# A recommendation tower on one core: one first load, a transposed batch in another PSUM bank, filler matmuls, layer 3 ahead of the dots, and gathers held behind lookups, dots and layer 1

## The reference, cut to what matters

```python
e = stack([tbl_0[ids[:, 0]], ..., tbl_25[ids[:, 25]]], axis=1)      # 512 x 26 x 128
sd = einsum('bfd,bd->bf', e, dense)
ss = einsum('bfd,bgd->bfg', e, e)
z = concatenate([dense, sd, ss[:, iu, ju]], axis=1)                 # pairs with f < g
h = concatenate([z, dense], axis=1)                                 # 512 x 607
h = maximum(h @ W_top1 + b_top1, 0.0)                               # 512 hidden
h = maximum(h @ W_top2 + b_top2, 0.0)                               # 256 hidden
y = h @ W_top3
```

## Time and profile before

| | us |
|---|---|
| median of 3 runs (lowest, highest) | 152.84 (150.93, 153.49) |
| time of the profiled execution | 151.2 |
| its span | 149.4 |
| mean granted TensorE clock | 0.886 |
| busy: PE, PE weight loads | 108.6, 95.6 |
| busy: DVE, ACT, POOL | 79.9, 66.7, 66.0 |
| DMA, mean over the span | 83 GB/s, 12.35 MB |

### The profile page before, as it was taken

The page is one execution under the profiler, slowest core; times in us unless marked ns, Lnnn a source line. Parts: engine busy times, 40 slices in busy tenths (PEclk is TensorE's granted clock), DMA queues, the critical chain, the costliest instruction groups (busy, mean ns, idle before and its releaser), DMA issues.

```text
span 149.4 us, 2760 instructions
## 1 busy us (share of the span) xinstructions
PE 108.6 (73%) x1074; PEld 95.6 (64%) x1074; DVE 79.9 (53%) x217; ACT 66.7 (45%) x151; POOL 66.0 (44%) x66
## 2 busy tenths in 40 slices
PE   7799961999999925500001957958997999799794
PEld 7588831888888805400001947948986998699782
DVE  5699919979999274000750020680386189248401
ACT  4463309737786053000502041693398288145620
POOL 7787747768787778777783752000000000000000
PEclk9999996599999996855555699996999999999999
DMA  4877961576999422111120211000000000000000
GB/s 116 257 193 188 247 191 36 175 183 199 305 287 249 153 53 53 53 53 53 35 52 19 57 35 42 2 0 4 4 0 0 4 0 0 4 4 0 0 0 1
DMA packets 5030, 12.35 MB, mean 83 GB/s; under 512 B 1725, under 2 KB 1853, under 8 KB 5018
## 3 DMA queue, kind: packets, MB, share of 16 engines
q1 hardware_dynamic: 3002, 8.09, 18.8%
q0 software_dynamic: 1920, 3.94, 10.3%
q10 hardware_dynamic: 96, 0.15, 0.4%
HBM read 12.18 MB, written 0.00 MB: 82 GB/s over the span
## 4 chain that ended last, share of the span: by engine, by line
PE 47%; issue 16%; DVE 14%; another core or an unknown queue 13%; ACT 9%; ACTq 0%
PE dots L443 19%; DVE pairs L347 12%; PE dots L487 12%; PE hidden L512 4%; PE hidden L542 3%; PE turned L467 3%; ACT embT L310 2%; ACT high L299 2%; PE dots L421 2%; ACT embT L285 2%; ACT pairs L285 2%; PE turned L512 1%; DVE embT L347 1%; PE last_layers L535 1%
## 5 line engine op out<-in xcount | busy, mean ns | idle before, releaser
L249 POOL DMA_INDIRECT rows<-tbl,gather_idx x60 | 63.3, 1055 | 24.2 <-issue 16.5
L354 DVE TENSOR_SCALAR onehot<-ids_h 125x512 fp32r<-125x512 f16 x88 | 33.4, 435 | 22.5 <-issue 13.9
L443 PE MATMUL dots<-onehot,high 125*128 125x512 f32 (+1 forms) x88 | 36.0, 426 | 0.0
L347 DVE COPY pairs<-dots 27x128 f32<-27x128 f32 (+8 forms) x88 | 23.7, 270 | 21.7 <-PE dots L487 19.1
L467 PE MATMUL turned<-ident,rows 128*128 128x128 f32 x60 | 10.8, 305 | 31.7 <-ACT embT L285 21.5
L443 PE MATMUL dots<-onehot,low 125*128 125x512 f32 (+1 forms) x88 | 32.9, 389 | 0.3 <-issue 0.3
L467 PEld LDWEIGHTS turned<-ident,rows 128*128 128x128 f32 x60 | 7.6, 154 | 34.8 <-issue 34.1
L285 ACT COPY pairs<-dots 27x128 f32<-27x128 f32 (+8 forms) x88 | 20.9, 237 | 18.6 <-PE dots L487 16.6
L299 ACT CAST high<-table 125x1024 fp32r<-125x1024 f32 (+1 forms) x12 | 11.6, 979 | 34.8 <-issue 14.3
L443 PEld LDWEIGHTS dots<-onehot,high 125*128 125x128 f32 x88 | 19.0, 216 | 3.1
L487 PE MATMUL dots<-embT 128*64 128x54 f32 x512 | 17.6, 234 | 3.7 <-DVE pairs L347 2.0
(11 more groups left out here) (43 smaller groups left out, 74.2 us busy)
## 6 DMA issues: line engine op xcount, KB each, us to landing
table<-tbl SPq DMA_DIRECT2D x10, 448.0 KB
wp<-w_pairs SPq DMA_DIRECT2D x2, 512.0 KB
rows<-tbl,gather_idx POOLq DMA_INDIRECT x60
table<-tbl SPq DMA_DIRECT2D x10, 52.0 KB
wd<-w_dense SPq DMA_DIRECT2D x1, 512.0 KB
w2s<-w SPq DMA_DIRECT2D x1, 512.0 KB
table<-tbl SPq DMA_DIRECT2D x2, 224.0 KB
denseT<-dense_t SPq DMA_DIRECT2D x1, 256.0 KB
```

Of the source, the lines that this page charges most:

```text
L249: pool.indirect_dma_start(out=rows[:, t % 2, n, :], out_offset=None, in_=tables[GATHERED_TABLES[n]][:, :], in_offset=bass.IndirectOffsetOn ...
L347: return nc.vector.tensor_copy(dst, src)
L354: nc.vector.tensor_scalar(onehot[:, i % 2, c, :], ids_h[:, i, :], float(c), None, ALU.is_equal).then_inc(onehot_ready, 1)
L443: last = nc.tensor.matmul(selected[t % 2][:, samples], part[:, t % 2, c, :], onehot[:, t % 2, c, samples], start=(part is high and c == 0) ...
```

## The change

- `spread` and the ids of the one-hots lie in one array, `first_needed`, and come with one DMA of 32 rows into one tile `first`; before there were two DMAs.
- Gathers: k = 9 to 41 wait for `table_selected` >= (k-6)//3. k = 42 and 46 also wait for the dots of tile 0, 51 and 54 for those of tile 1, 57 for layer 1 of tile 0. The waits on `transposed` in tiles 2 and 3 stay.
- Batch B2.2 (`APART`) is transposed into `last_layers` instead of `turned`, as soon as table 9's second half has been placed, and goes ahead of D1, as does a step W14 of 14 dummy matmuls. B2.3 and B3.0 move up one place too. `PLACERS` gives batches B2.0, B2.2, B3.0, B3.2, B3.3 to DVE (before: B2.0, B2.3, B3.2, B3.3).
- Y0 goes from behind D2 to ahead of it, Y1 from behind D3 to ahead of it.
- DVE fills `pairs` with ones after the sum of the dense weights in step T10, before at the start.
- The dummy matmuls write `last_layers` instead of `hidden[0]`.

```diff
+SPREAD_WORDS = len(ONEHOT_TABLES) * ROW_PARTS // 2 + 1
...
-    GATHERS_AHEAD, GATHERS_PER_TABLE = 7, 3
+    GATHERS_AHEAD, GATHERS_PER_TABLE = 6, 3
+
+    LATER_GATHERS = GATHERS_AHEAD + GATHERS_PER_TABLE * (N_ONEHOT + 1)
+    HELD_BY_DOTS, HELD_BY_LAYER1 = {42: 1, 46: 1, 51: 2, 54: 2}, {57: 2}
...
-        ids_i = sb("ids_i", [ID_ROWS, BATCH], I32)
+        first = sb("first", [128, BATCH + SPREAD_WORDS], I32)
+        ids_i = first[0:ID_ROWS, 0:BATCH]
...
-        spread_f = sb("spread_f", [128, N_ONEHOT, ROW_PARTS], F16)
+        spread_f = first[:, BATCH:BATCH + SPREAD_WORDS].bitcast(F16)
...
-            T10.0 B2.0 T9.3 T9.4 D0 C0.0 T10.1 T10.2 T10.3 T10.4 C0.1 P0 B2.1 P1
-            D1 C1.0 B2.2 L0.0 L0.1 R0 C1.1 B2.3 M0
-            B3.0 D2 C2.0 Y0 B3.1 L1.0 L1.1 R1 C2.1 P2 B3.2 M1
-            B3.3 D3 C3.0 Y1 L2.0 L2.1 R2 C3.1 P3 M2
+            T10.0 B2.0 T9.3 T9.4 D0 C0.0 T10.1 T10.2 T10.3 T10.4 C0.1 P0 B2.1 P1 W14 B2.2
+            D1 C1.0 B2.3 L0.0 L0.1 R0 C1.1 B3.0 M0 Y0
+            D2 C2.0 B3.1 L1.0 L1.1 R1 C2.1 P2 B3.2 M1 B3.3 Y1
+            D3 C3.0 L2.0 L2.1 R2 C3.1 P3 M2
             L3.0 Y2 L3.1 R3 M3 Y3""".split()]
 
-        PLACERS = [0, 0, 0, 0, 0, 0, 0, 0, 1, 0, 0, 1, 0, 0, 1, 1]
+        PLACERS = [0, 0, 0, 0, 0, 0, 0, 0, 1, 0, 1, 0, 1, 0, 1, 1]
+
+        APART = 2 * BATCHES + 2
...
-                    behind = (t * N_GATHERED + n - GATHERS_AHEAD) // GATHERS_PER_TABLE
-                    if t < 2 and behind > 0:
-                        pool.wait_ge(table_selected, behind)
+                    k = t * N_GATHERED + n
+                    if GATHERS_AHEAD + GATHERS_PER_TABLE <= k < LATER_GATHERS:
+                        pool.wait_ge(table_selected, (k - GATHERS_AHEAD) // GATHERS_PER_TABLE)
+                    if k in HELD_BY_DOTS:
+                        pool.wait_ge(dots_done, HELD_BY_DOTS[k])
+                    if k in HELD_BY_LAYER1:
+                        pool.wait_ge(layer1_done, HELD_BY_LAYER1[k])
...
+        def transposes_of(n):
+            return last_layers[:, :].rearrange("p (a b) -> p a b", a=BATCH_T) if n == APART else turned
...
-                 turned[:, 0:n, :]).then_inc(batch_placed[engine], 1)
+                 transposes_of(batch_no(t, b))[:, 0:n, :]).then_inc(batch_placed[engine], 1)
...
-            act.dma_start(spread_f[0:ID_ROWS, :, :], spread).then_inc(spread_loaded, 16)
-            act.dma_start(ids_i[:, :], onehot_ids).then_inc(onehot_ids_loaded, 16)
+            act.dma_start(first[0:ID_ROWS, :], first_needed).then_inc(first_needed_loaded, 16)
...
+                        nc.vector.memset(pairs[0:32, :, :, :], 1.0).then_inc(pairs_filled, 1)
...
-            nc.vector.memset(pairs[0:32, :, :, :], 1.0).then_inc(pairs_filled, 1)
...
+            def warm(count):
+                for _ in range(count):
+                    nc.tensor.matmul(last_layers[:, 0:128], zeros[:, :], zeros[:, :], start=True, stop=True)
+
             def step(kind, t, i=0):
-                if kind == "table" and i == 0:
+                if kind == "warming":
+                    pe.wait_ge(table_placed, N_ONEHOT + 1)
+                    warm(t)
+                elif kind == "table" and i == 0:
...
-                    if n >= 1:
-                        placer = batch_placer(n - 1)
-                        pe.wait_ge(batch_placed[placer], placed_by(placer, n))
+                    if n == APART:
+                        pe.wait_ge(table_placed, N_ONEHOT + 1)
+                    elif n >= 1:
+                        previous = n - 2 if n == APART + 1 else n - 1
+                        placer = batch_placer(previous)
+                        pe.wait_ge(batch_placed[placer], placed_by(placer, previous + 1))
...
                     if t == 0:
-                        pe.wait_ge(table_placed, N_ONEHOT + 1)
+                        placer = batch_placer(APART)
+                        pe.wait_ge(batch_placed[placer], placed_by(placer, APART + 1))
```

More of the change, by code:

```diff
@@ L44, with dlrm_tower @@
 PAIR_COPIES += [(3, 0, 12, 1, 4, 16), (2, 0, 3, 1, 4, 8), (0, 0, 0, 2, 2, 3)]
-def dlrm_tower(nc, gather_ids, onehot_ids, spread, tables, dense_t, w_pairs, w_dense, small, w2, identity,
+def dlrm_tower(nc, gather_ids, first_needed, tables, dense_t, w_pairs, w_dense, small, w2, identity,
                out):
@@ L118, in dlrm_tower @@
         ident_loaded = sem("ident_loaded")
-        spread_loaded = sem("spread_loaded")
-        onehot_ids_loaded = sem("onehot_ids_loaded")
+        first_needed_loaded = sem("first_needed_loaded")
         first_loaded = [sem(f"first_loaded{i}") for i in range(2)]
@@ L235, in _ @@
         def _(pool):
-            for first, last in ((ID_ROWS, 64), (64, 128)):
-                nc.gpsimd.memset(spread_f[first:last, :, :], 0.0).then_inc(spread_padded, 1)
+            for start, end in ((ID_ROWS, 64), (64, 128)):
+                nc.gpsimd.memset(spread_f[start:end, :], 0.0).then_inc(spread_padded, 1)
             pool.wait_ge(gather_ids_loaded, 16)
@@ L329, in step @@
                                          bias=b2s[:, 0:1]).then_inc(h2_ready[0], 1)
-            act.dma_start(spread_f[0:ID_ROWS, :, :], spread).then_inc(spread_loaded, 16)
-            act.dma_start(ids_i[:, :], onehot_ids).then_inc(onehot_ids_loaded, 16)
+            act.dma_start(first[0:ID_ROWS, :], first_needed).then_inc(first_needed_loaded, 16)
             act.wait_ge(zeros_ready, 1)
             nc.scalar.activation(warmed[:, :], zeros[:, :], ACT.Identity)
-            act.wait_ge(onehot_ids_loaded, 16)
-            nc.scalar.copy(ids_f[0:ID_ROWS, :], ids_i[:, :]).then_inc(ids_converted, 1)
+            act.wait_ge(first_needed_loaded, 16)
+            nc.scalar.copy(ids_f[0:ID_ROWS, :], ids_i).then_inc(ids_converted, 1)
             relate_ids(0)
@@ L416, in spread_ids @@
                     pe.wait_ge(spread_padded, 2)
-                    pe.wait_ge(spread_loaded, 16)
+                    pe.wait_ge(first_needed_loaded, 16)
                     pe.wait_ge(ids_converted, 1)
@@ L420, in spread_ids @@
                     pe.wait_ge(ids_relative, i - 1)
-                nc.tensor.matmul(relative[i % 2][0:ROW_PARTS, :], spread_f[:, i, :], ids_f[:, :], start=True, stop=True
+                nc.tensor.matmul(relative[i % 2][0:ROW_PARTS, :], spread_f[:, ROW_PARTS * i:ROW_PARTS * (i + 1)],
+                                 ids_f[:, :], start=True, stop=True
                                  ).then_inc(ids_spread, 1)
+            def warm(count):
+                for _ in range(count):
+                    nc.tensor.matmul(last_layers[:, 0:128], zeros[:, :], zeros[:, :], start=True, stop=True)
             def step(kind, t, i=0):
-                if kind == "table" and i == 0:
+                if kind == "warming":
+                    pe.wait_ge(table_placed, N_ONEHOT + 1)
+                    warm(t)
+                elif kind == "table" and i == 0:
                     if t + IDS_AHEAD < N_ONEHOT:
@@ L462, in step @@
                     pe.wait_ge(gathered[t % 2][i], 16 * BATCH_SIZE[i] * (t // 2 + 1))
-                    if n >= 1:
-                        placer = batch_placer(n - 1)
-                        pe.wait_ge(batch_placed[placer], placed_by(placer, n))
+                    if n == APART:
[4 more added lines that the diff above has]
+                        pe.wait_ge(batch_placed[placer], placed_by(placer, previous + 1))
                     for m in range(BATCH_SIZE[i]):
-                        last = nc.tensor.transpose(turned[:, m, :], rows[:, t % 2, BATCH_T * i + m, :],
+                        last = nc.tensor.transpose(transposes_of(n)[:, m, :], rows[:, t % 2, BATCH_T * i + m, :],
                                                    ident[:, :])
@@ L539, in _ @@
             pe.wait_ge(zeros_ready, 1)
-            def warm(count):
-                for _ in range(count):
-                    nc.tensor.matmul(hidden[0][:, 0, :], zeros[:, :], zeros[:, :], start=True, stop=True)
             warm(WARMING)
@@ L582 @@
     padded = np.concatenate([w1, np.zeros((1, HIDDEN1), w1.dtype), bias])
-    spread = np.zeros((ID_ROWS, N_ONEHOT, ROW_PARTS), np.float16)
+    spread = np.zeros((ID_ROWS, 2 * SPREAD_WORDS), np.float16)
     for i in range(N_ONEHOT):
-        spread[i, i, :] = 1.0
-    spread[N_ONEHOT] = np.arange(0, -ONEHOT_ROWS, -ROW_CHUNKS)
+        spread[i, ROW_PARTS * i:ROW_PARTS * (i + 1)] = 1.0
+        spread[N_ONEHOT, ROW_PARTS * i:ROW_PARTS * (i + 1)] = np.arange(0, -ONEHOT_ROWS, -ROW_CHUNKS)
     order = np.arange(BATCH).reshape(-1, 2, TILE // 4).transpose(0, 2, 1).reshape(-1)
     ids = ids[order]
-    onehot_ids = np.zeros((ID_ROWS, BATCH), ids.dtype)
+    onehot_ids = np.zeros((ID_ROWS, BATCH), np.int32)
     onehot_ids[0:N_ONEHOT] = ids[:, ONEHOT_TABLES].T
@@ L595 @@
         "gather_ids": ids[:, GATHERED_TABLES].reshape(TILES, TILE, N_GATHERED).transpose(1, 0, 2),
-        "onehot_ids": onehot_ids,
-        "spread": spread,
```

(4 more changed lines are left out.)

2 lines of the change are left out of this document (1 added, 1 removed).

## The result

After: 139.7 us median (139.26 to 140.23, four runs), before 151.88 (149.25 to 153.49, four runs), ratio 0.931, interval 0.9205 to 0.9414. The change is faster by 12.2 us, and 123.8 (115 to 134) had been predicted: the direction was right, the size was not. The profiled execution took 139.66 us with a span of 136.9.

What follows compares the result with a forecast made beforehand. PE was taken to stand because its signals are held while POOL issues gathers on end. 151.2 - 29.8 (holds) + 5.7 (late signals) - 1.2 (first hold) - 1.6 (fillers) - 0.5 (layer 3) = 123.8 us, range 115 to 134.

Steps and rivals of the forecast that it cites:

- The mechanism: PE's signals are held up while POOL issues gathers on end, released at the latest 1.9 to 2.0 us after it stops.
- T8's signal: Ahead of D0: with holds this lookup's signal comes at 53.1, so D0 ends at 64.8 instead of 94.61, 29.8 us less.
- Rival C: Whole kernel: PE's signals are late for PE's own reason, holds do nothing; 148 us, or 150; chance 0.08.
- Rival D: Lookups: late signals need longer POOL pauses, pace 4.2 us plus pause per release; slower, 162 at 4 us; chance 0.03.
- each worth up to 1.9 us: Late signals expected at T7, D0 and D1, together +5.7 us; bounds 0 and 15 us.
- Rival B: Dots: nine free gathers after D0 hold T10.4's signal, D1 8.6 us later, perhaps again at D2; 129 to 138; chance 0.17.
- the piece of 6.6: From T10.0's last products to D0's end: B2.0, T9.3, T9.4 and D0, priced at 6.6 us.
- First hold and first load, -1.2: Start: gather 12 waits for T1, POOL stops one gather earlier, -1.2 us; the single load's gain is swallowed.
- Fillers, -1.6: Ahead of D1: fillers and moved B2.2 keep the clock up, D1 3.90 instead of 5.51 us; -1.6 us.
- Layer 3, -0.5: Final chain: Y1 moves from between D3 and layer 1 to under DVE's last placing; -0.5 us.
- Y0 and B3.0 ahead of D2: Y0 waits for `h2` there, B3.0 waits for one placing less; both set at 0, bounds 0.5 either way.

Runs made afterwards that it cites:

- 13: Kernel before with only the new waits of the gathers, on a chip with late signals: 138.54 us.
- 9: Changed kernel with gathers 42 to 59 left out, on a chip with late signals: 126.53 us.
- 11: Changed kernel with POOL memsets in place of gathers 42 to 59, on a chip with late signals: 126.95 us (kernel before 153.81).
- 12: Changed kernel with plain DMAs from SP in place of gathers 42 to 59, on a chip with late signals: 127.41 us (kernel before 153.81).
- 7: Kernel before with only the new waits of the gathers, on a chip with signals on time: 113.96 us.
- 5: Changed kernel as it is, against the kernel before, on a chip with signals on time: 114.58 us against 113.0, ratio 1.011.
- 16: Changed kernel with closer holds, five gathers ahead, gather 57 held by layer 1 of tile 1, no W14 fillers; signals on time: 116.69 us.
- 18: Changed kernel with closer holds, five gathers ahead, gather 57 held by layer 1 of tile 1, no W14; signals on time: 115.01 us (before 113.84).
- 8: Kernel before, unchanged, run for its trace on a chip with late signals: 149.74 us.
- 10: Changed kernel with later gathers held closer (42 behind D0, 47 D1, 50 layer 1 of tile 0, 54 D2), late signals: 133.4 us (before 151.97).
- 1: Kernel before with gathers 30 to 59 left out, on a chip with signals on time: 114.74 us (before 112.71).
- 6: Changed kernel with the old waits of the gathers, on a chip with signals on time: 126.21 us.
- 15: Changed kernel with closer holds, five gathers ahead, gather 57 held by layer 1 of tile 1; signals on time: 128.65, 116.32, 128.41, 128.09 us.
- 17: Changed kernel with the old waits of the gathers, repeated on a chip with signals on time: 125.78 us.

## Why the prediction was wrong

- **The mechanism was right as far as it went.** Gathers issued on end hold PE's signals, and a hold lets them out. T8's signal is on time, 13 shows that the holds do it alone, 9, 11 and 12 that it is the gathers. How a gather does it isn't shown. Rival C is out. Against it stood the sentence of the Trainium skill ("SBUF — State Buffer", Who interferes with whom) that PE never waits on anyone; on late chips it can't be carried over from SBUF ports, of which that section speaks, to PE's pace as a whole: with gathers D1 takes 11.3 us, without them 4.2. Whether a port has a part in it, no run here shows. Rival D is out too: its pace of 4.2 us and a pause for each lookup didn't set in.
- **The step that failed is "each worth up to 1.9 us", at T7, at D0 and at D1.** I had priced a late signal by its release, 1.9 us after POOL stops, and PE's own work at nothing. T7's signal fits that (1.4 us). The two others don't: the signals of D0 and D1 themselves came on time (dots done at 70.57 and 88.65, copied from 70.60 and 88.68). In their place D1's matmuls crawled, 11.3 us instead of 4.2 in 9, and the relu's signal was 4.8 us late (92.7 to 97.51), with 1.2 more for the stretch up to D2's end (9.6 us from the relu, 8.4 in 9), whose first part runs at a granted clock of 0.50. The release is only the end of the lateness: a signal raised early in a free run is late by the rest of the run too (B2.2's, behind nine gathers, by 7.3 us, 76.63 to 83.89). Only the last signal of a run costs what I wrote. Of the 15.9 us that were missing, 9.9 are here (+5.5 and +4.4, each beyond a term of 1.9).
- **Rival B was nearer, with the wrong carrier.** It had the place (nine free gathers behind D0, "perhaps once again at D2") and 132 for one such loss; with two of its 8.6 us in place of the sum's 1.9 at D0 and at D1 it would have been 123.8 + 17.2 - 3.8 = 137.2. But T10.4's signal, which it named, was on time (ACT copied it at 73.60, after its own copies of dots), and P1 didn't wait. D1's own matmuls crawled, which no case had, since I took the rows to say "a late release, not a slow matmul". That its number comes near 139.7 is in part luck. A chance of 0.17 was too low: I had weighed against it that POOL starts rested. POOL had stood for 4.4 us (66.45 to 70.84), and only the first gathers behind it did no harm: T10.4's signal, 1.8 us into the run, was on time, PE kept its pace beside five gathers, and the crawl came with the sixth. Behind D1 layer 1's signal, 3.8 us into the run, was late already.
- **The end of D0: +5.1.** T10.0's signal, for which the sum had nothing, was 3.5 us late, and PE stood for it for 2.9 (60.64 to 63.50). D0 then took 7.07 us where the piece of 6.6 has 5.1 for it (89.53 to 94.61): 2.0 more. After the pause PE ran at the lower clock (0.52 up to 69.60), against D3's 3.94 at full clock a cost of 3.1 us, and a term the sum didn't have. In after such a stretch follows the waits at D1 and D2 too: 0.50 from 83.60 to 85.00 and from 98.00 to 102.00. The rest is less exact; in 9 to 13 D0 takes 8.0 to 8.4 us from its first matmul to its last, with single matmuls between, since it starts while gathers still run.
- **First hold and first load, -1.2: 0.2.** T1's signal did come earlier, at 20.53 on ACT instead of 22.41. But PE's stall behind T2 ends at 25.21, against 25.44 before, since ACT now saw B0.0's transposes, recorded done at 15.6, only at 24.01, and POOL stopped 1.77 us for T2's signal (done at 19.5, seen at 26.55). On prompt chips rows of tile 1 land late in after's variants and not in 7.
- **Fillers, -1.6: not on its own.** On the late chip it was buried under the crawl. On prompt ones the gain is there (1.56 in 5 against 7), and it is there without fillers too (16, 18). The price was taken from one execution, and 8 shows that it can be 0.
- **Layer 3, -0.5: right.** From D3 to the end 16.8 became 16.3, here and on the prompt chip (16.84 and 16.27). Y0 and B3.0 ahead of D2, set at 0 with bounds of 0.5, cost 0.35 (D1 to D2 12.46 in 5, 12.11 in 7).
- **Outside the span** 2.8 us instead of 1.8, in one profiled execution each; the other three runs of after have 1.8 to 2.5, and 139.7 holds either way. It isn't chance: every run of the kernel before has 1.8, most runs of after and its variants have 2.4 to 3.0 (some 1.8 to 2.0). Which part does it, is open.

## What to carry to other kernels

Where a run of one engine's work holds up another's signals, price a signal by how long the run still goes on after it, plus its release, and plus the lower clock after the pause, and ask whether the other engine's work crawls too. By the reading of 10, a hold pays when it keeps a run shorter than the time in which the consumers have other work; here that is the 6.6 us of copies behind each D, five gathers of 1.25. And before a kernel is tuned to such an effect, run it on more than one chip: here the same kernel stood some 40 us apart on two kinds of them, and the change that won 7% on the one lost about 1% on the other.

## What the runs showed of the hardware that was not expected

- The same kernel takes 113 us on some chips and 149 to 154 on others (or at other moments, which isn't separated). Nearly all of the difference lies ahead of the end of D0, where PE's signals are late: that end comes at 94.67 in 8, on a late chip, and at 58.26 and 57.36 in 1 and 7, on prompt ones.
- On late chips, back-to-back indirect DMAs of POOL (128 rows each, 0.95 us and 0.30 between) let PE record single matmuls, 0.7 to 1.4 us apart, in a stretch that runs 128 in 4.2 us without them (9). Memsets of POOL of the same length and SP's DMAs into the same tile don't. Why some chips do it and others not is open, and so is whether the descriptors or the fetches of rows do it.
- A single indirect DMA can take 11.39 us instead of about 1 beside DVE's work without a gap, and end 0.82 us after that work does (6, 15, 17); the kernel takes 12 to 15 us longer with it. That DVE's work is the cause is argued.
